# A megakernel over eight batches: every engine's list of work units in a new order, with a new allotment of PSUM banks

## The reference

```
x = layernorm(x);  xr = rmsnorm(x)
S6 scan:      h[t] = exp(dt[t]*A) * h[t-1] + dt[t]*u[t]*B[t]   for 16 states; y = sum over states of h*C
chunk attention in 2 chunks of 256 keys with silu gates;      x = x + norm(...)
gated FFN 128 -> 384 -> 128 (silu);                           x = x + norm(...)
16-head causal attention over 512 keys, head size 8;          x = x + norm(...)
twice: windowed attention (8 heads of 64, window 64, l2-normed and rotated q and k),
       then layernorm and a gated FFN 128 -> 341 -> 128 (gelu)
out = x + layernorm(...)
```

## Time and profile before

| | |
|---|---|
| three runs | 1775.11, 1777.71, 1778.22 us, median 1777.71 |
| the profiled execution | 1777.72 us, its span 1775.9 us (1.8 us lie around it) |
| busy | PE 1521.8 us (86%), DVE 1257.2 (71%), ACT 1255.0 (71%), POOL 368.7 (21%) |
| chain that ended last | PE 47%, ACT 26%, DVE 22%, issue 4%, POOL 1% |
| table loads | 113 on ACT |
| mean granted clock of PE | 0.93 |

### The profile page before, as it was taken

How to read it: one execution, slowest core, us unless ns; L and a number is a source line. 1 busy time by engine, 2 the same in 40 slices (tenths; PEclk the granted TensorE clock), 3 DMA queues, 4 the chain that set the end, 5 groups by cost and what they waited for, 6 DMA issues and landing times.

```text
span 1775.9 us, 30591 instructions
## 1 busy us (share of the span) xinstructions
PE 1521.8 (86%) x11892; PEld 840.5 (47%) x11892; DVE 1257.2 (71%) x2201; ACT 1255.0 (71%) x2867; POOL 368.7 (21%) x221
## 2 busy tenths in 40 slices
PE   3656788989989889889989899889998898998997
PEld 1212443344546444345456444555345554555664
DVE  6898958565576777888687886778775774366653
ACT  5533664568868487588898577874879965788895
POOL 2000000003044131022053002331111432035440
PEclk8788898789999989889999899999999988999999
DMA  6664206001323014123103143012320130010100
GB/s 241 243 234 148 71 12 133 4 6 37 64 54 53 22 58 125 45 82 102 33 22 85 61 149 78 22 44 56 109 96 16 22 85 9 1 30 22 22 20 18
DMA packets 70976, 121.51 MB, mean 68 GB/s; under 512 B 6864, under 2 KB 28240, under 8 KB 69072
## 3 DMA queue, kind: packets, MB, share of 16 engines
q1 hardware_dynamic: 70832, 119.55, 23.9%
HBM read 89.24 MB, written 15.60 MB: 59 GB/s over the span
## 4 chain that ended last, share of the span: by engine, by line
PE 47%; ACT 26%; DVE 22%; issue 4%; POOL 1%; DMA 0%; SPq 0%; ACTq 0%; DVEq 0%; POOLq 0%
ACT tiles L1584 7%; PE psum L602 5%; ACT L1418 4%; PE psum L843 4%; DVE neg_max L1190 3%; ACT tiles L1625 3%; DVE tiles L1112 3%; PE psum L673 3%; PE psum L875 2%; PE psum L983 2%; PE psum L826 2%; PE psum L830 2%; PE psum L876 2%; PE psum L803 2%; PE psum L807 2%
## 5 line engine op out<-in xcount | busy, mean ns | idle before, releaser
L1746 POOL TENSOR_TENSOR tiles<-tiles 128x1024 f32<-128x1024 f32 x64 | 155.8, 2434 | 778.6 <-DVE tiles L1369 778.6
L602 PE MATMUL psum<-cst,tiles 128*128 128x128 f32 x1408 | 208.7, 285 | 72.8 <-DVE tiles L1330 29.3
L1584 ACT ACTIVATE tiles<-psum,lmax,invn 128x128 f32<-128x128 f32 x512 | 226.5, 473 | 20.3 <-DVE lmax L1240 17.7
L602 PEld LDWEIGHTS psum<-cst,tiles 128*128 128x128 f32 x1408 | 162.4, 146 | 145.0 <-issue 99.0
L1190 DVE TENSOR_REDUCE neg_max<-psum 128x2 f32<-128x768 f32 (+3 forms) x176 | 189.9, 1122 | 48.5 <-PE psum L807 48.0
L673 PE MATMUL psum<-tiles,cst 128*128 128x512 f32 x256 | 144.3, 696 | 41.3 <-DVE tiles L1116 41.3
L1757 POOL TENSOR_TENSOR tiles<-tiles,lsum 128x1024 f32<-128x1024 f32 x64 | 127.7, 1995 | 236.3 <-DVE lsum L1244 236.3
L1112 DVE TENSOR_TENSOR_SCAN tiles<-tiles 128x512 f32<-128x512 f32 x128 | 162.8, 1306 | 4.3 <-ACT tiles L1477 1.8
L1418 ACT ACT_TABLE_LOAD x113 | 145.0, 1283 | 2.7 <-PEq L1958 0.7
L1477 ACT ACTIVATE tiles<-tiles,colp 128x512 f32<-128x512 f32 x128 | 89.6, 724 | 74.0 <-DVE tiles L1112 66.1
L1528 ACT ACTIVATE tiles<-psum 128x768 f32<-128x768 f32 (+1 forms) x128 | 114.8, 926 | 28.8 <-PE psum L830 25.2
(11 more groups left out here) (227 smaller groups left out, 3385.0 us busy)
## 6 DMA issues: line engine op xcount, KB each, us to landing
tiles<-bc_scratch SPq DMA_DIRECT2D x128, 512.0 KB, 4.8
v_prev<-tiles SPq DMA_DIRECT2D x112, 128.0 KB, 2.3
split_scratch<-tiles SPq DMA_DIRECT2D x96, 128.0 KB, 2.4
tiles<-split_scratch SPq DMA_DIRECT2D x32, 384.0 KB
wts<-in_wts SPq DMA_DIRECT2D x1, 3114.0 KB, 15.5
tiles<-in_x SPq DMA_DIRECT2D x8, 256.0 KB, 3.1
out<-tiles SPq DMA_DIRECT2D x8, 256.0 KB, 2.4
tiles<-in_rowp SPq DMA_DIRECT2D x1, 768.0 KB, 7.5
```

Of the source, the lines that this page charges most:

```text
L602: ins = nc.tensor.transpose(ps[:, j * 128:(j + 1) * 128], src[:, j * 128:(j + 1) * 128], ident)
L1584: ins = fn(pr[:, i * 128:(i + 1) * 128], ps[:, i * 128:(i + 1) * 128], ACT.Exp, bias=own(lmax)[:, b, i:i + 1], scale=own(invn)[:, j, 0, 2 ...
L1746: tt(T(TURNED, 2), T(TURNED, 2), T(TURNED + 2, 2), ALU.add).then_inc(sem("qk_sum"), 1)
```

## The change

Only the texts in `ORDER` and `BANKS` are replaced. The units, their instructions and their number are the same; every engine's list has as many entries as before. The new order was fitted to lengths of the units taken from a trace. In the diff below the parts spoken of later are kept: the beginnings of the lists, and the stretch of PE's list with the `row_scores` units of batches 1 and 0.

```diff
     "PE": (
-        "10000010110200100210380000380120020120230020330130210430310500400510610720400630420500730510810920600830620700930710a10c"
...
-        "00n00l00p10s00q10t10u10v10w00m00o30g00r20f20e20d30h30i30j20g00s00t00u00v00w10y10x11011110z11211b11e11c11h11d11g11i11f117"
-        "11a11811911511411611300x00y01100z11j01201001h01f01d11k11l11n01i11m11o11q11s11p11w11r11t11v01e01c11u11x11y11z12130k123120"
...
+        "80010010110210380100000100230000310430130210520030320120220300410610700500630430510820410900720500830630710a20610c10b009"
+        "10f10e10d20710g00a10h30810i10j30900c00b10k20810l10n10p00f00e10m10o10q00d30a10r00g30c30b20900h30f00i30e30d00j20a10s30g10t"
+        "10u10w10v20c20b30h20f30i20e20d30j00k20g00l00n00p00m00o00q20h00r20i10y10x10z11011220j11111f11g30k30l11d11e30n00s11h11c00t"
+        "11b00u00v11i11a11400w30p30m30o11930q11511311711611830r11j00y11k11l11n30s00x11m11o11q11s11p11r11v11t11w00z01011u30t11x11y"
...
     "DVE": (
-        "10000080280080510110200100280710300380380180680410410500400510600610700720080920180820230020330130230310810a10910b204205"
...
+        "80280080580780380180610080410110210310410510680910700080820000100230020120200330130210810930320310a10b10c10d10e00410f005"
...
     "ACT": (
-        "80080110000010110210200100210300310410500400510600610710800700810910a10b00900a00b20020120230030120330220420530320610d30410c"
...
+        "80080110010110210310410510610710810910a10b00020000100230020130100330220210c00400510d30300610e10f00730400830520300900a00b"
...
     "SP": (
-        "10000080480180680780880080280580380980a20080b101001300102103002003201301104105202004302203005303106107204006304205007305"
...
+        "80480180680780880080280580380910080a00020080b101300102103001002104105301003201004302303106202107005203006304305108204109"
...
 BANKS = (
-    "010210230000121020112340404400410440401041041010340110210121023023014201003012406460460460460426426426044062406026042024"
...
+    "000100001010121213121340454400000240240242404245244024501020120121041023230460323502250742045740257474074624020024601536"
...
```

More of the change, by code:

```diff
@@ L201 @@
[L201 to L212, removed]
@@ new lines @@
+        "01h12s20l01c12t01i01420n01a20p01301620m01520o01920q01701812u20r12v12w13501j30y30x30z31031231112x12y13412z01k01l01n01m01o"
+        "01q01s13601p01r01v13013113701t13d13801w01u13201x01y13e01z02102313f02002602213a13902413g13m13h02702513302813b13n02a20s029"
+        "13c13o02c02b13j13i13p02d02e02h13q02f02i13k02g02j02k02l02n13l02p13s13r02m02o13t02q20t13u02r20v13v02s31f31g13w02t13x31e20u"
+        "20w31d31b14214314014113y13z31c31h31i02u14402v14502w03514614714g31a31402x31302y03402z14914814f14a31603703603d14h31514c14b"
@@ new lines @@
+        "14i14o03103014j03814d14p03g03f03m14q14e03214k14l14r03e03303a03914s14x03h14m14y03b03o14n14u14t03p03n03c14z14v31703j03i150"
+        "03q15114w03k31931820y03l03s03r31j20x03t20z15315203u21203v15431k31l03w15531n31m15603x31o15731q31p15831r04204304004115b15c"
+        "15d15e15915a03y03z15f04431s31v04531w31t21021131u31x04604704g31y31z32132032204832304904f32404a50032632550132732950221f328"
+        "04h04b04c04i04o04j04d04p04e32a32c50332e32b32d04q32i04k04l04r32f04x04s04m04y04n32h32g32k21e21d32j04z32l32m05032n32p04u04t"
@@ new lines @@
+        "32o32q05104v32r21g21h04w32s50421c21b05305205421i50505521421a05605705832t50605b05c05d05e05905a21621750705f21332u50832w335"
+        "32v50921521932x32y50a33450c40032z40140250b21840333633733d21j33133033833250f50e33e33350d21k21l33f33a33933g50g21m33h33m21o"
+        "33b33n21n21q21s33c21p21r33o21t33j33i21v21w21u33p21y33k21x33q21z22133l22022322222640422422740522822a33s33r22c22522933t22e"
+        "22b22d22h22f22i33u40633v22j22l33w22n22g22k40722m22o22p40822q50h33x22r50i40950j34234334034133y33z40a34422s22t40c34540b346"
@@ new lines @@
+        "34734g50k50l50n40f40e50p22u50m34850o34934f34a22v50q22w23540d50r34i34h34o34b34c34j22x34d22y34p34e40g23422z34r34q34x34k34l"
+        "34s50s34m34y23723650t23123023d34z50v34t34u35050u23850w35134n23f34v23223g23m34w23a23923e23323h40h35235340i35423b23n40j23o"
+        "35523j23i23c23k35623p50y35723q23l35850x50z51051251123s23r35b35c35d35e35935a51f51d51e35f51g51b51h51c51i51451a515517519513"
+        "51651823t40k23u40l40n40p40m23v70040o23w70170240q51j70340r23x24224351k51l51n24024170451m51o51q23y70523z51p51r51s40s51t51v"
@@ new lines @@
+    "230213215327037041602071201201201014061436075231702302572537057601204646240263420276746062450705701034603013555351655345"
+    "123526351555635775731733567376516076531463601450277205775602764071350350112764726424612315733372312317211772117344707123"
+    "403460324372302342326360276476601210345635013203432673032736462367306706757601031256315073475670247024602640240267674576"
+    "546574575767024607513620303503452240520264062424201235030030150563170176071357073015736734702762352702157023707245475623"
@@ new lines @@
+    "764673604220140630162004620457240230210204754675627051706376750240672640267062023052302375606030623520300360360613641613"
+    "063012032100162106076527656062406314014204201351635156031024240540560241621406402045160120134560534246760123614013630610"
+    "340264060460460246246702457465462402301431317501371751310230530357402702757434702576324327607236734763623623501210275120"
+    "731072302573742701402327364076367106054354263024562762023724650246757627076546724564504576237467560543524563245023027265"
@@ L335 @@
+    "23570725672325702172057237425647076754247607601476076071231207161012010210201201271701723021730120")
 class Waiting:
```

207 lines of the change are left out of this document (96 added, 111 removed).

## The result

| | before | after |
|---|---|---|
| median of 8 runs each (lowest to highest) | 1777.3 us (1774.97 to 1778.22) | 1788.6 us (1781.1 to 1793.87) |
| ratio, 95% interval | | 1.006 (1.0049 to 1.0071) |
| profiled execution | 1777.72 us | 1790.59 us |

The new order is **slower by 0.6%**, 11.3 us by the medians and 12.9 by the two profiled executions. The forecast was a gain of 15. The result lies in the range (1732 to 1790), on the other side of zero.

What follows compares the result with a forecast made beforehand. The prediction saw no single engine as the bound, but a long chain of handovers between engines. Its terms, −12.8 − 12 + 5.0 + 4.5 = −15.3 us, took 1777.7 to 1762 us, range 1732 to 1790.

Steps and rivals of the forecast that it cites:

- Runs of score units: Three stretches with long `row_scores` runs: breaking the runs gives TensorE other work and removes its idle time there, −12.8 us.
- The clock: Stretches at 286 to 345 and 725 to 775 us: part of the time at half clock comes back, −12 us.
- Table loads: ScalarE's list: function set changes rise from 113 to 120, 55% of each load on the path, +5.0 us.
- The start: Inputs of batches 1 and 0 behind constants, statistics behind preparation: `xr` of batch 1 up to 6 us late, +4.5 us.
- All else: Over a thousand units changing places with near neighbours: waits removed come back elsewhere, set at 0, bounds −65 and +80.
- The slower rival: Banks for `lqk_in` asked for too early, so TensorE waits 28 us more: 1790 us, chance 0.23.
- nothing to measure: Whole kernel: old order perhaps as well fitted, waits only change places, later batches pay back broken runs: 1778 us, chance 0.13.
- larger gain: Whole kernel: lists fit real lengths everywhere, winning half the way to the best stretch, 32 us: 1743 us, chance 0.14.

Runs made afterwards that it cites:

- The hybrids there: Two kernels switching order where both had done the same units: new order first, then old, 1790.81 us; old first, then new, 1780.5 us.
- mid_new: Kernel before with the new order's lists from 420 to 1460 us only, old order on either side: 1874.22 us, ratio 1.0548.
- end_new: Kernel before with its old lists up to 1440 us, then the new order: 1790.34 us, ratio 1.0082.
- start_new: New lists up to 408 us, then all the rest in the order of the kernel before: 1794.47 us, ratio 1.0112.

## Why the prediction was wrong, by its own steps

**Runs of score units, −12.8 us: this step failed.** It took the idle time of three stretches as gone, since TensorE's list is the longest. The waits for the maxima did shrink, by 8.3 us in all, and around batch 2's score units TensorE is now nearly full (566 to 640 us: 70.36 of 74 busy). But TensorE waits for something else instead. In the first part it was batch 0's queries and keys, 9.0 us in one wait: from 283 to 331 us, where nine tenths were foretold, it is busy for 35.51 of 48 us. In the middle it was `qk_turned`, 13.0 us more than before. All three priced stretches lie in the first half, and there TensorE's idle time did not fall by 12.8 us, it rose by 13.8, from 168.1 to 181.9 for the same units. After 200 us it rose from 167.1 to 172.0 where about 150 were foretold. The step named what the broken run would stop waiting for, and never what the inserted units would.

**The clock, −12 us: mis-sized, and of the wrong sign over the kernel.** A mean clock of c says that 2 × (1 − c) of a stretch was at the lower level. Up to 400 us that is 136 us before and 92 after, of which 16 us of the fall lie in the first 200, where nothing was priced; the instructions of the first part are 10.6 us shorter. But over the whole first half, with the same units done, only 2.1 us of this are left, and in the second half the instructions are 8.0 us longer. Summed over the six stretches from 400 to 1600 us the time at the lower level was 108 us and is now 156. The remark that a dip can reappear elsewhere was in the text and cost only a point of size; it should have been the value. The mean clock is 0.928 where 0.95 was foretold; single executions of the kernel before lie between 0.923 and 0.932, so against its 0.93 nothing has moved.

**Table loads, +5.0 us: mis-sized by a little.** 0.96 us per added load instead of 0.71 makes 6.7 us for seven. The Trainium skill's figure ("ScalarE: Activation LUTs", What ACT_TABLE_LOAD costs), 2.66 us for every switch, is not borne out: the earlier trace rows shows no drain at a switch (the load starts at 9.74 and takes 1.28, the next activation starts at 11.04), the kernel's reaction to an added load (a reload, not a switch) stays below the 1.283 us of the load alone, and 20 switches taken away brought 0.58 us each. The line's share of the chain is 4.3%, under the 4.8 foretold. And the added loads do not explain the middle part: counted in the three parts there are 33, 25 and 55 before, 39, 24 and 57 after.

**The start, +4.5 us: wrong in sign.** `xr` of batch 1 came at 22.92 instead of 26.7 or later. (The 23.1 of its sum should read 23.0, 24.85 − 1.83.) I had kept the old duration of the wait for the constants and only put the statistics behind it; without two inputs ahead of them the constants landed earlier, and `tables` began at 13.66. The new kernel is 5.9 us ahead at work 100. VectorE is busy for 172.0 of the first 200 us, 171.6 before, so that check says neither.

**All else, 0: this step failed too.** It held over a thousand moves, and with the broken runs it is where the loss lies: 7.3 us ahead at work 200, the new order is 11.7 behind at the clean cut. The hybrids there put 13 us of net loss into the first half of the kernel and some 3 into the second. The later stretches, from 1400 us on, where the prediction looked for the loss, are not to blame: TensorE idles 31 us there and did 37 before. That it might cost was known; that a stretch with no priced term could outweigh the two priced ones was given too little weight.

**The slower rival** named its mechanism rightly and its size wrongly. Waits of TensorE on line 1369 grew by 8.0 us, to 19.6, just under the 20 that were to show it, against the 28 of its sum. By the traces these waits took the place of those for `row_max`, over the whole kernel one for one, in the middle part with 4.7 us on top. That they are the reason is read from the traces, and no run took them away alone. The rival **nothing to measure**, with its sentence that waits only change places, describes the waits for banks best, as they hardly changed in sum. For the **larger gain** there is nothing: TensorE's idle time rose.

**What stays open:** which of the moves of the first half starts the loss. Batch 2's score units begin 31 us earlier (579 instead of 610 us), yet the last of them ends 6 us later (765 instead of 758) and its first `exps` start 15 us later (787 instead of 772), so work was begun early and ended late; whether that is cause or consequence was not tried. So the place of the loss, the first half, and its kind, waiting, are shown; which units' places cause it is not. Nor is it known why the single executions of the kernel after spread over 0.7% and those of before over 0.2%.

## What to carry to other kernels

Price a new order by what TensorE will wait for next, not only by the waits that it removes; compare two orders only at points where both have done the same units, since any other cut divides the loss wrongly; and set a clock dip that is broken up to come back elsewhere unless a row says otherwise. The lists of the engines, of the transfer queue and of the banks are fitted to each other: a part of a new order cannot be tried or taken alone (every cut with a misfit cost 19 to 42 us, read from the lags: from +49.6 to +92.0 at the costliest seam of `mid_new`, from −0.6 to +18.3 at that of `end_new`), unless the cut lies where all engines have done the same units. A small move inside a fitted order, here groups of one table set put together for at most 3.5 us of delay, was the only thing that paid, and further moves with longer delays did not add to it.

## What the runs showed of the hardware that was not expected

- A table load whose set is loaded already costs its full time: with 23 of them ScalarE is busy for 1286.6 us instead of 1255.0, 31.6 for 23 × 1.283 = 29.5, and the kernel takes 22.0 us longer.
- Once two kernels are in the same order, the lag between them stays the same to a few tenths of a microsecond for over a thousand (`start_new`: +17.4, +17.9, +18.1, +18.2), clock dips included. In the six stretches of 200 us from 550 us on the granted clock was 0.92, 0.97, 0.94, 0.97, 0.94, 0.99 in the kernel before, and the same six numbers stand in `start_new` from 568 us on: here the clock followed what TensorE was given to do, in another kernel as well.
- TensorE was at its lower clock, 1.2 GHz, for a seventh of a kernel in which it is busy 86% of the time (mean granted clock 0.93) and in which, after 200 us, only three of its waits are longer than 3 us. A new order moved these times about and left their sum nearly as it was (0.928).
